# Gate and up products of the last stage as three fp16 products instead of one fp32 product

## The chip, the cores and the metric

The kernel runs on one core of one Trainium2 chip. The metric is the device time of one launch in microseconds (us); lower is better. Before the change the median of three runs is 945.73 us (944.59 to 948.35). "Before" is the kernel without the change, "after" the one with it.

## The reference, cut to what matters

A pre-norm decoder block over two sequences of 512 tokens of width 1024: a first attention with sign weights, a second attention (16 heads of 16 features, causal) inside a block that keeps four channels per feature, and a dense layer with adapters. The change touches the middle of the second block:

```
mlp_in = rat_read(hidden_states, mlp_read_w, g, b, 2)        # layer-normed reads
g_in, u_in = mlp_in[..., :H], mlp_in[..., H:]                # H = 256
gate = einsum('bli,oi->blo', g_in, ctx[0])                   # 256 -> 1024
up   = einsum('bli,oi->blo', u_in, ctx[1])                   # 256 -> 1024
mlp_out = silu(gate) * up
hidden_states = rat_write(hidden_states, mlp_out, ...)
```

All inputs and outputs are fp32.

## The kernel before, in words

The 1024 tokens are 8 tiles of 128. Three stages matter here. The *second attention* (lines 1859 to 1920 on TensorE, 1033 to 1048 on ScalarE, 1402 to 1443 on VectorE) runs 8 rounds of 16 score tiles: TensorE makes scores (L1860), VectorE takes their maxima (L1406), TensorE makes them again shifted (L1904), ScalarE takes the exponential (L1037), GpSimd masks (L779), TensorE sums with the values (L1915). The *last stage* then handles the 8 token tiles one after the other, software-pipelined: in the round of tile i, the "first" half makes the write of the attention result of tile i, the read and the gate and up products of tile i; the "second" half makes the write of the MLP result of tile i-1; "dense" makes the dense layer of tile i-2.

Order on each engine is program order; waits are counting semaphores. In the round of tile i of the last stage:

- TensorE: `products_1` (L1942), `products_2` (L1949), the dense layer's pieces (L1988, L1992, L2041, L2048, L2069), the transposes `turn_state` (L1822, region_p) and `turn_read` (L1822, yn), the read (L2001), and `gate_up` (L2013): 32 fp32 products of 128x128 weights (`ctx_w`) with 128 columns of the turned read `ynT`, each of which the trace shows as two records.
- ScalarE: among others `read_turned` (L1055, four copies with scale and shift that make `ynT`), then `decays` (L1025) of the write of tile i-1, then `gate`: a table load (L1059), the tanh (L1061), a table load (L1062).
- GpSimd: `read_root_2` (L797), `write` of tile i-1: `write_a` (L766) and `write_h` (L771, which waits for `decays`), then `dense_root` (L801); the write of the next tile and `attended` (L756) follow.
- VectorE: the read's statistics and normalisation (L1531 to L1539), the write of tile i-1 (`write_end`: L1474 to L1499, where L1493 waits for `decays` and L1499 for `write_h`), `gated` (L1546, after the tanh; L1549, after the up product), `to_dense` (L1554 to L1563), then the write of the next tile with L1517 in it; its last instruction, L1499, releases `turn_state`.

Tiles 0 and 1 are handled ahead of the steady rounds (2 to 7); after them come two rounds without a "first" half.

Of the kernel before, what the change touches and what calls it, by code (L numbers as in the profile page):

```python
# [103 lines left out]
def build_program(nc, d, out):  # L104
    ctx = ExitStack()
    with ctx:
# [89 lines left out]
        ctx_w = region_w[:, _o:_o + 4 * M].rearrange("p (w k n) -> p w k n", w=2, k=2)  # L196
# [41 lines left out]
        h_0 = c_o[:, 0:D]  # L238
        h2T = ops[:, 4 * S:8 * S].bitcast(F32).rearrange("p (c n) -> p c n", c=KC)
# [55 lines left out]
        def run_rounds(eng, round_):  # L295
# [69 lines left out]
        y2_step, y2_rstd, y2n_ready = sem("y2_step"), sem("y2_rstd"), sem("y2n_ready")  # L365
        y2T_mm, y2T_ready, gu_mm, tanh_ready, mlp_ready = (sem(n) for n in (
            "y2T_mm", "y2T_ready", "gu_mm", "tanh_ready", "mlp_ready"))
        f_step, f_rstd, xf_ready = (sem(n) for n in ("f_step", "f_rstd", "xf_ready"))
# [280 lines left out]
        def _(pool):  # L649
# [148 lines left out]

            def dense_root(i):
                pool.wait_ge(f_step, 5 * i + 5)  # L800
                pool.tensor_tensor(rstd[:, 0, :], ves[:], minus_half[:, 0:1], ALU.pow).then_inc(f_rstd, 1)  # L801

            read_root_2(0)
            write(0, 1, h_in)
            attended(2)
            read_root_2(1)
            write(1, 0, h_0)
            dense_root(0)
            for i in range(2, NT + 1):
# [5 lines left out]
                write(1, i - 1, h_mid[(i - 1) % 2])  # L815
                dense_root(i - 1)
# [3 lines left out]
        def _(act):  # L820
# [209 lines left out]

            act.preload_act_table_set("natural_log_exp_and_others")
            for i in range(XI):
                for n, (kt, j) in enumerate(X_PROB_TILES):
                    if i > 0 and n % 8 == 0:
                        act.wait_ge(xpv_done, 2 * i - 1 + n // 8)
# [16 lines left out]
            def read_turned(i):  # L1052
                act.wait_ge(y2T_mm, i + 1)
                for n in range(4):
                    act.activation(ynT[:, n, :], psum[:, 7, n * P:(n + 1) * P], ACT.Identity,  # L1055
                                   scale=cols[:, g2 + n:g2 + n + 1], bias=cols[:, b2 + n:b2 + n + 1]).then_inc(y2T_ready, 1)

            def gate(i, bank):
                act.preload_act_table_set("exp_and_others")  # L1059
                act.wait_ge(gu_mm, 2 * i + 1)  # L1060
                act.activation(mlpT_f.rearrange("p (h n) -> p h n", h=2), psum[:, bank:bank + 2, :], ACT.Tanh, scale=0.5).then_inc(tanh_ready, 1)  # L1061
# [49 lines left out]
        def _(dve):  # L1111
# [300 lines left out]

            def x_invert(b):
# [87 lines left out]
            for i in range(XI):  # L1501
                for n in range(16):
# [5 lines left out]
                    if (i, n) == (5, HEAD_INVERT):  # L1508
                        x_invert(0)
            to_state(0, h_0)  # L1510
# [32 lines left out]
            def gated(i, bank=0):  # L1543
# [5 lines left out]
                dve.scalar_tensor_tensor(t2, t2, 0.5, psum[:, 6:8, :], ALU.mult, ALU.mult).then_inc(mlp_ready, 1)  # L1549
# [60 lines left out]
        def _(pe):  # L1610
# [397 lines left out]
            def gate_up(i, bank):  # L2008
                pe.wait_ge(y2T_ready, 4 * i + 4)
# [142 lines left out]
```

## Time and profile before

| what | us |
|---|---|
| median of 3 runs | 945.73 |
| the profiled execution, its time | 947.53 |
| its span, first to last instruction | 945.8 |
| TensorE busy | 834.6 (88%) |
| VectorE busy | 648.4 (69%) |
| ScalarE busy | 418.0 (44%) |
| GpSimd busy | 305.9 (32%) |

The mean granted clock of TensorE is 0.934 of its full 2.4 GHz. The second attention lies between about 530 and 629 us of the span, the last stage from there to the end; the steady rounds begin their gate and up products at 705.99, 741.94, 777.88, and so on to 885.57 us, 35.9 us apart. PE is TensorE, PEld its weight loads, DVE VectorE, ACT ScalarE, POOL GpSimd.

### The profile page before, as it was taken

Reading aid. Unit: us, or ns where it says so; the run is one execution under the profiler, and the core shown is the slowest. Engines: PE = TensorE matmul, PEld = TensorE weight load, DVE = VectorE, ACT = ScalarE, POOL = GpSimd, SP = SyncE. Lnnn points to the kernel's source line nnn. Section 1 sums busy time; section 2 is a strip of 40 time slices with the busy share of each in tenths; the row PEclk is TensorE's granted clock in tenths of the full one; section 3 lists DMA queues with packets and bytes.
Section 4 is the critical chain, followed back from the end, with each engine's and each line's share of the span. In section 5 each row is a group of like instructions: output and inputs, shape, how many; then the busy total and the mean of one; then the engine's idle time right before and its main releaser. Section 6 shows DMA issues by size and latency. Waiting matters only on the chain.

```text
span 945.8 us, 15035 instructions
## 1 busy us (share of the span) xinstructions
PE 834.6 (88%) x5594; PEld 450.7 (48%) x5594; DVE 648.4 (69%) x1348; ACT 418.0 (44%) x819; POOL 305.9 (32%) x297
## 2 busy tenths in 40 slices
PE   4899689999999999899996778877799999999977
PEld 2675233333343333356664323236556656656633
DVE  7865367787887874467786667435678778679661
ACT  4466415676676767223343356533232332332310
POOL 2000004676676767310100135342232232232210
PEclk9899799999999999999997578768799999999997
DMA  8664522141322222111225431110001001001011
GB/s 329 235 231 137 167 73 90 60 111 47 108 79 77 88 67 96 57 45 42 79 68 167 182 97 59 47 43 17 1 1 47 16 30 45 10 35 34 7 38 45
DMA packets 75625, 75.78 MB, mean 80 GB/s; under 512 B 37493, under 2 KB 63877, under 8 KB 74918
## 3 DMA queue, kind: packets, MB, share of 16 engines
q1 hardware_dynamic: 74998, 68.77, 23.8%
q10 hardware_dynamic: 560, 6.12, 1.7%
q8 instruction: 41, 0.67, 0.3%
q14 instruction: 26, 0.21, 0.1%
HBM read 53.56 MB, written 21.04 MB: 79 GB/s over the span
## 4 chain that ended last, share of the span: by engine, by line
PE 67%; DVE 11%; ACT 7%; DMA 5%; SPq 4%; issue 4%; POOL 2%; POOLq 0%; DVEq 0%; ACTq 0%; PEldq 0%
PE psum L1625 6%; PE psum L1707 6%; PE psum L2013 6%; PE psum L1988 5%; PE psum L1758 5%; PE psum L1747 5%; PE psum L1949 4%; PE psum L1815 4%; PE psum L1822 3%; PE psum L1768 3%; PE psum L1915 3%; DMA ops<-q_scr 2%; SPq L536 2%; PE psum L1893 2%; PE psum L2001 2%
## 5 line engine op out<-in xcount | busy, mean ns | idle before, releaser
L1271 DVE TENSOR_REDUCE m_neg<-psum 128x1 f32<-128x512 f32 x256 | 164.5, 682 | 43.6 <-PE psum L1707 41.6
L911 ACT ACTIVATE region_x<-psum 128x512 f32<-128x512 f32 x256 | 140.8, 596 | 64.0 <-PE psum L1747 63.8
L679 POOL TENSOR_TENSOR region_p<-region_x 128x2048 f32<-128x2048 f32 x32 | 145.3, 4539 | 42.0 <-ACT region_x L911 25.7
L1707 PE MATMUL psum<-ops 96*128 96x512 f16 x256 | 97.0, 387 | 13.1 <-DMA ops<-q_scr 11.8
L1747 PE MATMUL psum<-ops 98*128 98x512 f16 x256 | 95.7, 381 | 1.7 <-ACT region_x L911 1.5
L1625 PE MATMUL psum<-region_x,region_w 128*128 128x512 f16 x320 | 77.0, 398 | 3.0 <-ACT region_w L849 3.0
L1707 PEld LDWEIGHTS psum<-ops 96*128 96x128 f16 x256 | 24.8, 97 | 93.5 <-DVE m_neg L1271 64.0
L2013 PE MATMUL psum<-ynT,region_w 128*128 128x128 f32 x512 | 63.5, 288 | 6.3 <-ACT ynT L1055 6.3
L1758 PE MATMUL psum<-region_x,v_g 128*32 128x512 f32 x512 | 67.8, 604 | 0.0
L2013 PEld LDWEIGHTS psum<-ynT,region_w 128*128 128x128 f32 x512 | 61.9, 203 | 10.0 <-ACT ynT L1055 10.0
L1815 PE MATMUL psum<-sign_o_all,region_a 128*128 128x512 f16 x256 | 60.2, 387 | 4.3 <-DVE region_p L1338 2.8
L1988 PE MATMUL psum<-region_a,c_o 128*128 128x512 f16 x256 | 59.3, 386 | 0.0
L1037 ACT ACTIVATE region_p<-psum 128x512 f32<-128x512 f32 (+2 forms) x96 | 39.2, 462 | 39.4 <-PE psum L1904 38.9
L1625 PEld LDWEIGHTS psum<-region_x,region_w 128*128 128x128 f16 x320 | 32.5, 102 | 45.7 <-issue 9.4
L1406 DVE CUSTOM_DVE_ANT_0 c_o<-psum,v_g 128x128 f32<-128x128 f32 (+3 forms) x86 | 39.2, 482 | 16.0 <-PE psum L1860 15.8
L779 POOL TENSOR_SCALAR_AFFINE_SELECT region_p<-region_p 128x128 f32<-128x128 f32 x96 | 27.9, 306 | 65.4 <-ACT region_p L1037 63.9
L1860 PE MATMUL psum<-ops 48*128 48x128 f16 (+3 forms) x128 | 36.9, 364 | 10.0 <-DVE m_neg L1406 8.5
L1949 PE MATMUL psum<-region_s,region_w 128*128 128x376 f32 x128 | 44.1, 490 | 1.5 <-DVE region_w L1549 1.5
L1904 PE MATMUL psum<-ops 50*128 50x384 f16 (+3 forms) x128 | 35.8, 367 | 10.6 <-ACT region_p L1037 6.0
L766 POOL TENSOR_TENSOR region_w<-sp_b 128x768 f32<-128x768 f32 x16 | 25.9, 1619 | 53.9 <-DVE sp_b L1474 53.9
L1815 PEld LDWEIGHTS psum<-sign_o_all,region_a 128*128 128x128 f16 x256 | 25.3, 100 | 31.8 <-DVE region_p L1338 3.0
L1988 PEld LDWEIGHTS psum<-region_a,c_o 128*128 128x128 f16 x256 | 24.8, 100 | 30.4 <-issue 4.3
(236 smaller groups left out, 1485.4 us busy)
## 6 DMA issues: line engine op xcount, KB each, us to landing
ops<-q_scr SPq DMA_DIRECT2D x48, 128.0 KB, 2.6
region_a<-in_x SPq DMA_DIRECT2D x8, 512.0 KB, 8.5
region_a<-in_w_q SPq DMA_DIRECT2D x8, 512.0 KB, 7.1
region_w<-in_w_o SPq DMA_DIRECT2D x8, 512.0 KB, 4.0
region_w<-in_kern SPq DMA_DIRECT2D x16, 256.0 KB, 2.9
kern_scr<-region_w SPq DMA_DIRECT2D x32, 128.0 KB, 1.9
region_p<-in_x SPq DMA_DIRECT2D x8, 512.0 KB, 3.6
region_a<-kern_scr ACTq DMA_DIRECT2D x1, 4096.0 KB
```

The source lines that it names most:

```text
L679: pool.tensor_tensor(pair_sum[:, n], prob_a[:, 2 * n], prob_a[:, 2 * n + 1], ALU.add).then_inc(pair_ready, 1)
L911: act.activation(prob_a[:, kt, j, :], psum[:, (0, 4, 5)[(16 * i + n) % 3], :], ACT.Exp, scale=A_SCALE).then_inc(p_ready, 1)
L1037: act.activation(prob_x[kt][:, j, :], psum[:, 4 + (16 * i + n) % 3, 0:S - kt * P], ACT.Exp, scale=X_SCALE).then_inc(xp_ready, 1)
L1271: dve.tensor_reduce(m_neg[:, i % 3, n:n + 1], psum[:, 1 + (16 * i + n) % 3, :], AX_X, ALU.max, negate=True).then_inc(s_max, 1)
L1625: mm = pe.matmul(psum[:, bank, 0:width], *((x[:, c, tokens], w) if swap else (w, x[:, c, tokens])), start=(c == 0 and part == 0), stop=(c ...
L1707: pe.matmul(psum[:, 1 + (16 * i + n) % 3, :], qa_op[u][0:A_MAX, j, qt * P:(qt + 1) * P], k_op[u][0:A_MAX, :], start=True, stop=True).then_ ...
L1747: pe.matmul(psum[:, (0, 4, 5)[(16 * i + n) % 3], :], k_op[u][0:A_ROWS, kt * P:(kt + 1) * P], qa_op[u][0:A_ROWS, j, :], start=True, stop=Tr ...
L1758: mm = pe.matmul(psum[j * 32:(j + 1) * 32, 6, :], v_g[:, i % 3, kt, :], prob_a[:, kt, j, :], start=(kt == 0), stop=(kt == QT - 1))
L1815: mm = pe.matmul(psum[:, h, :], (o_in_hi, o_in_lo)[n % 2][:, n // 2, ds(i * P, P)], sign_o[:, n // 2, h * 512:(h + 1) * 512], start=(n == ...
L1949: mm = pe.matmul(psum[:, 2, 0:N_W], mlpT[:, c, :], write2[:, c, :], start=(c == 0), stop=(c == KC - 1))
L1988: pe.matmul(psum[:, 4 + h, :], fT_hi[:, c, :], kern[:, w, c, h * 512:(h + 1) * 512], start=(c == 0 and w == 0), stop=False)
L2013: mm = pe.matmul(psum[:, at + f // 4, (f % 4) * P:(f % 4 + 1) * P], ctx_w[:, n, k, f * P:(f + 1) * P], ynT[:, 2 * n + k, :], start=(k == 0 ...
```

## The change

The weights of the gate and up products are split into two fp16 parts, high (times 64, rounded) and low (the rest), during rounds 2 to 5 of the second attention: 8 copies on ScalarE and 8 subtractions on VectorE of 128x512 each. The turned read is made in two fp16 parts as well: ScalarE writes the high part straight from PSUM (4 instructions) and then the fp32 form (the 4 that were there), and GpSimd subtracts the one from the other (`read_lo`, one instruction of 128x512). `gate_up` is then 96 fp16 products: 64 with the high part of the read (against the weights' high and low parts), and 32 with its low part (against the weights' high part). The semaphore for gate comes after the 16th of the last 32, that for up at the end. The factor 64 is taken out in the tanh's scale and in `gated`.

On GpSimd, in a steady round, `read_lo` stands behind both parts of the write. Before:

```order
L797 TENSOR_TENSOR rs<-ve,minus_half 128x2 [waits y2_step]
L766 TENSOR_TENSOR region_w<-sp_b 128x768 [waits sp_ready_2]
L771 TENSOR_TENSOR region_w<-region_p,region_w 128x768 [waits abar_ready_2]
L801 TENSOR_TENSOR rstd<-ves,minus_half 128x1 [waits f_step]
L766 TENSOR_TENSOR region_w<-sp_b 128x768 [waits sp_ready_1]
```

and after, at the same place:

```order
L801 TENSOR_TENSOR rs<-ve,minus_half 128x2 [waits y2_step]
L770 TENSOR_TENSOR region_w<-sp_b 128x768 [waits sp_ready_2]
L775 TENSOR_TENSOR region_w<-region_p,region_w 128x768 [waits abar_ready_2]
L806 TENSOR_TENSOR lo_st<-ynT,hi_st 128x512 [waits gu_mm,y2T_ready]
L810 TENSOR_TENSOR rstd<-ves,minus_half 128x1 [waits f_step]
L770 TENSOR_TENSOR region_w<-sp_b 128x768 [waits sp_ready_1]
```

L806 is new; `abar_ready_2` is what `decays` of the MLP write releases. On ScalarE the same round has this before (L1055 makes the turned read, L1025 is `decays`):

```order
L1055 ACTIVATE ynT<-psum,cols 128x128 [waits y2T_mm]
L1055 ACTIVATE ynT<-psum,cols 128x128 x3
L1025 ACTIVATE region_w<-region_w 128x768 [waits da_ready_2]
L1059 ACT_TABLE_LOAD
L1061 ACTIVATE region_w<-psum 128x1024 [waits gu_mm]
```

and this after:

```order
L1080 ACTIVATE hi_st<-psum,cols 128x128 [waits y2T_mm]
L1080 ACTIVATE hi_st<-psum,cols 128x128 x3
L1080 ACTIVATE ynT<-psum,cols 128x128 x4
L1038 ACTIVATE region_w<-region_w 128x768 [waits da_ready_2]
L1084 ACT_TABLE_LOAD
L1086 ACTIVATE region_w<-psum 128x1024 [waits gu_mm]
```

`decays` now stands behind four more instructions. On TensorE the two rows of `gate_up`, `L2013 ... [waits y2T_ready]` and its 31 followers, become 96 products; around the place where the low part of the read comes in, after:

```order
L2046 MATMUL psum<-hi_st,ops 128x128 x2
L2046 MATMUL psum<-hi_st,region_w 128x128 x2
L2046 MATMUL psum<-lo_st,ops 128x128 [waits y2_lo_ready]
L2046 MATMUL psum<-lo_st,region_w 128x128
L2046 MATMUL psum<-lo_st,ops 128x128
```

The row with `y2_lo_ready` is the 65th product; the wait is new. The diff, cut to its core:

```diff
@@ -193,7 +193,8 @@
...
         ctx_parts = region_w[:, _o:_o + 4 * M].rearrange("p (w n) -> p w n", w=4)
-        ctx_w = region_w[:, _o:_o + 4 * M].rearrange("p (w k n) -> p w k n", w=2, k=2)
+        _ctx = [ops[:, XI * 2 * S:(XI + 2) * 2 * S], ctx_parts[:, 0, :].bitcast(F16), ops[:, (XI + 2) * 2 * S:(XI + 4) * 2 * S], ctx_parts[:, 1, :].bitcast(F16)]
+        ctx_hi, ctx_lo = ([c[:, n * M:(n + 1) * M] for c in _ctx] for n in range(2))
@@ -236,6 +237,7 @@
...
         h_0 = c_o[:, 0:D]
+        y2_hi, y2_lo = (t[:].rearrange("p (c n) -> p c n", c=4) for t in (hi_st, lo_st))
@@ -363,8 +365,10 @@
...
         y2_step, y2_rstd, y2n_ready = sem("y2_step"), sem("y2_rstd"), sem("y2n_ready")
+        CTX_TILES = {(i + 2, n): (i, n // 8) for i in range(4) for n in (3, 11)}
...
             "y2T_mm", "y2T_ready", "gu_mm", "tanh_ready", "mlp_ready"))
+        ctx_hi_ready, ctx_lo_ready, y2_lo_ready = (sem(n) for n in ("ctx_hi_ready", "ctx_lo_ready", "y2_lo_ready"))
@@ -796,15 +800,22 @@
...
 
+            def read_lo(i):
+                pool.wait_ge(y2T_ready, 8 * i + 8)
+                pool.wait_ge(gu_mm, 2 * i)
+                pool.tensor_tensor(y2_lo, ynT[:, 0:4, :], y2_hi, ALU.subtract).then_inc(y2_lo_ready, 1)
+
...
             read_root_2(0)
+            read_lo(0)
...
             write(1, 0, h_0)
+            read_lo(1)
@@ -813,6 +824,8 @@
...
                 write(1, i - 1, h_mid[(i - 1) % 2])
+                if i < NT:
+                    read_lo(i)
@@ -1028,9 +1041,20 @@
...
 
+            def split_ctx_hi(c, h):
+                if (c, h) == (0, 0):
+                    act.wait_ge(xw_loaded, 16 * 6)
+                if h == 0 and c % 2 == 0:
+                    act.wait_ge(xst_mm, 16 * (c + 2))
+                if c % 2 == 1:
+                    act.wait_ge(ctx_lo_ready, 2 * (c // 2) + 2)
+                act.activation(ctx_hi[c][:, h * 512:(h + 1) * 512], ctx_parts[:, c, h * 512:(h + 1) * 512], ACT.Copy, scale=F_GAIN).then_inc(ctx_hi_ready, 1)
+
...
                 for n, (kt, j) in enumerate(X_PROB_TILES):
+                    if (i, n) in CTX_TILES:
+                        split_ctx_hi(*CTX_TILES[i, n])
@@ -1051,14 +1075,15 @@
...
                 act.wait_ge(y2T_mm, i + 1)
-                for n in range(4):
-                    act.activation(ynT[:, n, :], psum[:, 7, n * P:(n + 1) * P], ACT.Identity,
-                                   scale=cols[:, g2 + n:g2 + n + 1], bias=cols[:, b2 + n:b2 + n + 1]).then_inc(y2T_ready, 1)
+                for to in (y2_hi, ynT):
+                    for n in range(4):
+                        act.activation(to[:, n, :], psum[:, 7, n * P:(n + 1) * P], ACT.Identity,
+                                       scale=cols[:, g2 + n:g2 + n + 1], bias=cols[:, b2 + n:b2 + n + 1]).then_inc(y2T_ready, 1)
...
                 act.wait_ge(gu_mm, 2 * i + 1)
-                act.activation(mlpT_f.rearrange("p (h n) -> p h n", h=2), psum[:, bank:bank + 2, :], ACT.Tanh, scale=0.5).then_inc(tanh_ready, 1)
+                act.activation(mlpT_f.rearrange("p (h n) -> p h n", h=2), psum[:, bank:bank + 2, :], ACT.Tanh, scale=0.5 / F_GAIN).then_inc(tanh_ready, 1)
@@ -1410,6 +1435,12 @@
...
 
+            def split_ctx_lo(c, h):
+                dve.wait_ge(ctx_hi_ready, 2 * c + h + 1)
+                part = slice(h * 512, (h + 1) * 512)
+                dve.scalar_tensor_tensor(ctx_lo[c][:, part], ctx_parts[:, c, part], F_GAIN, ctx_hi[c][:, part],
+                                         ALU.mult, ALU.subtract).then_inc(ctx_lo_ready, 1)
+
@@ -1507,6 +1538,8 @@
...
                         x_invert(0)
+                    if (i, n - 4) in CTX_TILES:
+                        split_ctx_lo(*CTX_TILES[i, n - 4])
@@ -1546,7 +1579,7 @@
...
                 dve.wait_ge(gu_mm, 2 * i + 2)
-                dve.scalar_tensor_tensor(t2, t2, 0.5, psum[:, 6:8, :], ALU.mult, ALU.mult).then_inc(mlp_ready, 1)
+                dve.scalar_tensor_tensor(t2, t2, 0.5 / F_GAIN ** 2, psum[:, 6:8, :], ALU.mult, ALU.mult).then_inc(mlp_ready, 1)
@@ -2006,12 +2039,24 @@
...
             def gate_up(i, bank):
-                pe.wait_ge(y2T_ready, 4 * i + 4)
-                for n, at in ((0, bank), (1, 6)):
+                pe.wait_ge(y2T_ready, 8 * i + 4)
+
+                def product(n, f, k, w, y, start, stop):
+                    at = (bank, 6)[n] + f // 4
+                    return pe.matmul(psum[:, at, (f % 4) * P:(f % 4 + 1) * P], w[2 * n + k][:, f * P:(f + 1) * P], y[:, 2 * n + k, :], start=start, stop=stop)
+
+                for n in range(2):
+                    for f in range(KC):
+                        if (n, f) == (1, KC // 2):
+                            pe.wait_ge(y2T_ready, 8 * i + 8)
+                        for k in range(2):
+                            product(n, f, k, ctx_hi, y2_hi, f % 4 == 0 and k == 0, False)
+                            product(n, f, k, ctx_lo, y2_hi, False, False)
+                pe.wait_ge(y2_lo_ready, i + 1)
+                for n in range(2):
...
                         for k in range(2):
-                            mm = pe.matmul(psum[:, at + f // 4, (f % 4) * P:(f % 4 + 1) * P], ctx_w[:, n, k, f * P:(f + 1) * P], ynT[:, 2 * n + k, :],
-                                           start=(k == 0), stop=(k == 1))
+                            mm = product(n, f, k, ctx_hi, y2_lo, False, f % 4 == 3 and k == 1)
@@ -2072,6 +2117,7 @@
...
             pe.wait_ge(made, 21)
+            pe.wait_ge(ctx_lo_ready, 8)
```

## Rows read from the trace of the kernel before

**Rows 1.** The page, part 1: busy us (share), instructions.

```profile
PE 834.6 (88%) x5594; PEld 450.7 (48%) x5594; DVE 648.4 (69%) x1348; ACT 418.0 (44%) x819; POOL 305.9 (32%) x297
```

**Rows 2.** Windows: length, busy of PE, PEld, DVE, ACT, POOL; PEclk, DMA share, GB/s.

```profile
740.00:892.00 152.00, 144.21 (x886) 96.42 (x884) 120.94 (x198) 51.03 (x92) 40.72 (x29) 1.00 0.10 26
```

**Rows 3.** Timeline of TensorE, a steady round: start, length, instruction, [idle before].

```profile
741.94 7.41 PE L2013 MATMUL psum<-ynT,region_w 128*128 128x128 f32 x64 [0.52 <-ACT ynT L1055]
749.19 0.81 PE L1992 MATMUL psum<-region_a,c_o 128*128 128x512 f16 x3
749.83 1.88 PE L2069 MATMUL psum<-region_w 65*128 65x512 f32 x4
...
768.19 1.04 PE L1822 MATMUL psum<-ident,region_p 128*128 128x128 f32 x8
```

**Rows 4.** Timeline of TensorE, sixteen fp16 products of 128 columns.

```profile
761.79 1.05 PE L2041 MATMUL psum<-c_o,region_w 128*64 128x128 f16 x16 [1.25 <-ACT c_o L1029]
```

**Rows 5.** Timeline of ScalarE, the same steady round.

```profile
740.38 1.51 ACT L1055 ACTIVATE ynT<-psum,cols 128x128 f32<-128x128 f32 x4 [5.15 <-PE psum L1822]
741.76 0.85 ACT L1025 ACTIVATE region_w<-region_w 128x768 f32<-128x768 f32 x1
...
745.81 1.02 ACT L1061 ACTIVATE region_w<-psum 128x1024 f32<-128x1024 f32 x1 [1.89 <-PE psum L2013]
```

**Rows 6.** GpSimd: timeline of two writes.

```profile
670.96 2.50 POOL L771 TENSOR_TENSOR region_w<-c_o,region_w 128x768 f32<-128x768 f32 x1 [1.47 <-ACT region_w L1025]
...
742.70 2.04 POOL L771 TENSOR_TENSOR region_w<-region_p,region_w 128x768 f32<-128x768 f32 x1 [1.02 <-ACT region_w L1025]
```

**Rows 7.** Groups of instructions by shape: busy us, mean ns, idle before.

```profile
L683 POOL TENSOR_TENSOR region_a<-region_w,region_a 128x512 f16<-128x512 f32 x14 | 16.3, 1161 | 24.0 <-ACT region_a L920 24.0
```

**Rows 8.** Timeline of VectorE: the write of tile 0, then the steady round.

```profile
670.91 0.96 DVE L1493 SCALAR_TENSOR_TENSOR region_w<-region_w 128x768 f32<-128x768 f32 x1
...
749.46 1.22 DVE L1549 SCALAR_TENSOR_TENSOR region_w<-region_w,psum 128x1024 f32<-128x1024 f32 x1 [0.79 <-PE psum L2013]
...
763.02 2.02 DVE L1493 SCALAR_TENSOR_TENSOR region_w<-region_w 128x768 f32<-128x768 f32 x1
...
766.06 0.96 DVE L1499 TENSOR_TENSOR region_p<-region_w 128x768 f32<-128x768 f32 x1
```

**Rows 9.** Timeline of TensorE, two idle gaps in dense work, and a window behind one.

```profile
387.80 3.63 PE L1815 MATMUL psum<-sign_o_all,region_a 128*128 128x512 f16 x16 [1.44 <-PEq L1828]
399.72 8.77 PE L1815 MATMUL psum<-sign_o_all,region_a 128*128 128x512 f16 x32 [2.83 <-DVE region_p L1338]
```

**Rows 10.** Windows, behind the second of these gaps (columns as in rows 2).

```profile
401.00:404.00 3.00, 3.00 (x8) 1.06 (x7) 2.24 (x6) 0.00 (x0) 0.55 (x1) 0.50 0.45 147
```

**Rows 11.** Groups by shape: splits of 128x512 weights in the first attention.

```profile
L924 ACT ACTIVATE region_w<-region_w 128x512 f16<-128x512 f32 x16 | 10.0, 624 | 2.2 <-DMA region_w<-in_kern 2.2
...
L1300 DVE SCALAR_TENSOR_TENSOR region_w<-region_w 128x512 f16<-128x512 f32 x16 | 11.4, 713 | 2.5 <-ACT region_w L924 2.5
```

**Rows 12.** Timeline of the second attention: idle of ScalarE and of VectorE.

```profile
578.34 0.49 ACT L1037 ACTIVATE region_p<-psum 128x384 f32<-128x384 f32 x1 [2.24 <-PE psum L1904]
...
572.26 0.42 DVE L1406 CUSTOM_DVE_ANT_0 c_o<-psum,v_g 128x256 f32<-128x256 f32 x1 [0.69 <-PE psum L1860]
...
578.12 0.29 DVE L1406 CUSTOM_DVE_ANT_0 c_o<-psum,v_g 128x128 f32<-128x128 f32 x1 [1.42 <-PE psum L1860]
```

**Rows 13.** Timeline, start of the last stage (DVE, PE).

```profile
642.50 0.47 DVE L1474 SCALAR_TENSOR_TENSOR sp_b<-region_w 128x304 f32<-128x304 f32 x1 [1.62 <-ACT region_w L1021]
...
652.93 5.32 PE L1949 MATMUL psum<-region_s,region_w 128*128 128x376 f32 x16 [1.46 <-DVE region_w L1549]
```

**Rows 14.** Timeline of TensorE behind the last gate and up products.

```profile
895.18 5.22 PE L1949 MATMUL psum<-region_s,region_w 128*128 128x376 f32 x16
...
922.22 1.97 PE L1822 MATMUL psum<-ident,region_p 128*128 128x128 f32 x8 [5.21 <-DVE region_p L1563]
...
925.36 1.91 PE L2041 MATMUL psum<-c_o,region_w 128*64 128x128 f16 x16 [1.17 <-ACT c_o L1029]
```

## The prediction, on record before the changed kernel ran

> **What bounds the kernel now.** I read the page first: TensorE is busy 88% of the span [rows 1]. Then the stage windows: over 152 us of steady rounds of the last stage it is busy 144.2 us, at full granted clock (1.00, that is 2.4 GHz) [rows 2]. So there a microsecond taken from TensorE counts only as far as nothing else comes late, and each wait put in front of it counts at once. Third, the timelines of the four engines through one steady round. I measure from G, the start of the gate and up products (741.94). They run from G to G+7.25, where the next instruction starts at 749.19 [rows 3]; ScalarE's four copies end at G [rows 5]; the tanh starts at G+3.87; VectorE ends L1549 at 750.68, G+8.74, and its last instruction, L1499, at 767.02 [rows 8], while TensorE asks for the result at 768.19 [rows 3]. VectorE has thus 1.15 us of room; TensorE sets the period, and the change adds a wait in its queue.
>
> **The products alone.** Sixteen fp16 products of 128 columns take 1.05 us [rows 4]. The end of such a run holds about 0.16 us in which the next may already go (7.41 against 7.25 in rows 3), so one costs (1.05 - 0.16)/16 = 56 ns. 96 cost 5.4 us against 7.25, 1.85 less per tile. The stationary side in rows 4 is 64 columns wide, here it is 128; the nearest rows with 128 are those of the old products, 7.41/64 = 116 ns a record. I take 56 and keep 116 as the other end.
>
> The Trainium skill ("TensorE: Matmul & The Clock Gate", Back-to-back issue gap) gives about 81 ns for a 128-column product with its own weight load, against 56 for an isolated one. No run here shows 128 weight columns at this size, and rows 4 are nearer to 56; by 81 the 64 products would end at G+5.2 and the whole at G+8.5, an estimate, with a much shorter wait in between and about the same total as my sum.
>
> **When the low part of the read is there.** Step by step, in a steady round:
> - ScalarE's four copies take 1.38 us from 740.38 to the start of L1025 at 741.76 [rows 5]; four more put that start at G+1.2 and its end (0.85) at G+2.1. The high part is ready at G, as the fp32 form was.
> - GpSimd's L771 waits for L1025. So does VectorE's L1493, which is free by then. This pair was released together once before: VectorE took 0.96 us and GpSimd 2.50 [rows 6, 8], while elsewhere it needs 2.04. So L771 ends at G+2.1+0.1+2.5 = G+4.7.
> - `read_lo` stands behind it and has the shape of L683, 1.16 us [rows 7]: ready at G+5.9.
>
> The skill ("SBUF — State Buffer", Who interferes with whom) says that only the port pair shared by VectorE and GpSimd collides, and that the lock is exclusive. The trace agrees: 2.50 us is about 0.96 + 1.6.
>
> **TensorE.** After 64 products it stands at G+3.6 and waits 2.3 us for G+5.9; 32 more take 1.8: the end is G+7.7 instead of G+7.25, +0.45. The 1.85 gained has turned into the wait. Queued behind the waiting product are L1992, L2069 and the next tile's `products_1`; all come 0.45 later. Over five periods between the six steady rounds: **+2.3**. As a lower bound (L771 at 2.04, nothing blocked) the low part is there at G+5.3 and the end is G+7.1: -0.15 a round.
>
> **VectorE.** The gate semaphore now comes 16 products after the low part: G+5.9+0.9+0.16 = G+7.0. The tanh (1.02, rows 5) ends at G+8.1, the two of `gated` (1.22 each) at G+10.6 instead of G+8.74: +1.9. It has 1.15 of room, and part of the delay is taken back at L1493 of the next write: at 763.02 it took 2.02 us, blocked by GpSimd's L771; coming later it meets less of it, up to 1.06 less. What is left of 1.9 is at most the 0.45 that TensorE is late anyway. **0** here.
>
> **Behind the last tile** no `products_1` stands between: L1949 starts at 895.18 = G+9.6 [rows 14] and waits for `gated`, now G+10.6: **+1.0**.
>
> **Start of the stage.** In the round of tile 0, GpSimd makes the low part at once, but L1474 waits for ScalarE's L1021 (642.50, idle 1.62) [rows 13], which stands behind the four new copies: +1.4 down to L1949 at 652.93. TensorE's products end earlier and its successor starts later, so its idle of 1.46 there becomes some 5 us. Behind the one gap of that size, 5.21 us, the granted clock was at its lower level: the eight transposes took 1.97 against 1.04 and L2041 1.91 against 1.05 [rows 14, 3, 4], 1.8 in sum. So **+3.2**; bounds 1.4 (clock held) to 4.5. In the round of tile 1 the wait for VectorE ends as late as before: 0.
>
> **Clock in the steady rounds.** The new gap is 2.3 us. A gap of 1.44 in dense work left 16 products at 3.63; after one of 2.83 the clock read 0.50 (1.2 GHz) and 32 of them took 8.77 instead of 7.1, 1.7 lost [rows 9, 10]. 2.3 lies between and nearer to the latter. I take three falls in six rounds: **+5.1**; bounds 0 and 10.2.
>
> **Second attention.** ScalarE gets 8 copies of 0.62 and VectorE 8 subtractions of 0.71 [rows 11]. ScalarE's stand where it waits 2.24 us for TensorE's sums [rows 12] (or half that, at the other place) and cost nothing; without that cover, 8 x 0.62 = 5.0. VectorE's stand behind its 8th and 16th tile of a round; its idle comes only a few tiles later (0.69 and 1.42, rows 12), so a score product that needs the next maximum waits some: I take 0.2 of 0.71 each, **+1.6**, bounds 0 and 5.7.
>
> **Sum.** 2.3 + 0 + 1.0 + 3.2 + 5.1 + 1.6 = 13.2 on the profiled execution's 947.53 gives 960.7. That execution stands 1.8 above the median of 945.73, so the median after is **959**, 1.4% slower. Without falls of the clock it is 954, with six 964.
>
> **Rivals.**
> - *The low part comes in time, faster.* Place: GpSimd in front of `read_lo`. The copies are complete at G+1.4; were GpSimd free then, the part would be there at G+2.6, before G+3.6, and TensorE would keep 1.85 in each of five periods: -9.3, with start and attention (+1.4, +1.6) 945.7 - 6.3 = about 939. It decides from the point where L771 ends before G+2.4, 2.3 us sooner than I work out. For it: GpSimd is idle most of the time (32%). Against: the order on GpSimd and ScalarE. Chance 0.07.
> - *The wait is short and the clock holds.* The lower bounds together: the part at G+5.3, gap 1.7, no fall, attention free: 945.7 + 1.4 + 0.5 - 0.8 = 947; up to 950 with a part of the rest. Chance 0.14.
> - *The products cost nearer to 116 ns.* 64 end at G+7.4, after the low part, so no gap and no fall; all 96 at G+11.1, +3.9 a round: 5 x 3.9 + 4 behind the last + 1.4 + 1.6 = 26.5, 972. For it: each product has a weight load of its own. Against: rows 4 have that too. Chance 0.07.
> - *The forecast*, a wait of about 2 us with or without falls, 951 to 968: 0.72.
>
> **Numbers.** Range 948 to 969. Half a per cent, 4.7 us, is about what a measurement of this kernel can tell. Faster by more: 0.07. Within: 0.14 (the second rival). Slower by more: 0.79.
>
> **What would show it.** In the profile after: a wait of TensorE for GpSimd's subtraction, 2.3 us, before the 65th product in each steady round; products 56 ns apart before it; L771 at about 2.5 us right in front of the subtraction; L1546 waiting for the tanh, which starts at G+7; periods of 36.4 us, and about 1.7 more where the granted clock reads 0.50 behind the gap; L1949 of tile 0 starting 1.4 later relative to its G. Wrong would be: no wait at the 65th product (the first rival), a spacing over 80 ns, or a second attention longer by more than 5 us.

## The result, and the profile after

The changed kernel takes 964.75 us (median of 4 runs, 962.37 to 966.32), the kernel before in the same session 945.16 (944.45 to 948.35): a ratio of 1.0173, 95% interval 1.0134 to 1.0212. A later session of six runs gave 1.0215 (1.0176 to 1.0254). The change makes the kernel about 2% slower. The profiled execution has a span of 964.0 us against 945.8, so 18.2 us more are to be found. A *fall*, below, is a stretch in which TensorE's granted clock reads 0.50 in the middle of dense work.

The first row of the page shows 256 matmuls more than [rows 1] and hardly more busy time:

```profile
PE 836.0 (87%) x5850; PEld 443.9 (46%) x5850; DVE 650.5 (67%) x1356; ACT 433.8 (45%) x859; POOL 319.4 (33%) x305
```

The same window of steady rounds as in [rows 2]: TensorE is busy for 136.4 us of 152 instead of 144.2, and its granted clock is 0.97 on average. It idles more, and some of its work runs slower.

```profile
740.00:892.00 152.00, 136.42 (x966) 86.08 (x965) 111.64 (x193) 51.28 (x101) 44.09 (x31) 0.97 0.10 26
```

One steady round, G = 751.12, where G is the start of the gate and up products as in the prediction. These rows are the counterparts of [rows 3, 5, 6, 8]. Line numbers are those of the changed kernel: L2046 the products, L1080 the copies, L1038 the decays, L775 `write_h`, which was L771, L806 `read_lo`, L1086 the tanh. In the kernels of the experiments the same instructions stand a few lines off (the products at L2045 in e_early, at L2049 in e_swapst). TensorE:

```profile
751.12 0.28 PE L2046 MATMUL psum<-hi_st,ops 128*128 128x128 f16 x2 [0.52 <-ACT hi_st L1080]
...
756.95 0.23 PE L2046 MATMUL psum<-lo_st,ops 128*128 128x128 f16 x1 [2.08 <-POOL lo_st L806]
757.02 0.22 PE L2046 MATMUL psum<-lo_st,region_w 128*128 128x128 f16 x1
...
758.16 0.31 PE L2046 MATMUL psum<-lo_st,region_w 128*128 128x128 f16 x1
758.26 0.31 PE L2046 MATMUL psum<-lo_st,ops 128*128 128x128 f16 x1
...
759.76 1.45 PE L2025 MATMUL psum<-region_a,c_o 128*128 128x512 f16 x3
```

ScalarE, VectorE and GpSimd in the same round:

```profile
749.56 1.50 ACT L1080 ACTIVATE hi_st<-psum,cols 128x128 f16<-128x128 f32 x4 [5.15 <-PE psum L1855]
750.95 1.52 ACT L1080 ACTIVATE ynT<-psum,cols 128x128 f32<-128x128 f32 x4
752.32 0.88 ACT L1038 ACTIVATE region_w<-region_w 128x768 f32<-128x768 f32 x1
...
758.29 1.02 ACT L1086 ACTIVATE region_w<-psum 128x1024 f32<-128x1024 f32 x1 [3.79 <-PE psum L2046]
...
753.23 0.96 DVE L1524 SCALAR_TENSOR_TENSOR region_w<-region_w 128x768 f32<-128x768 f32 x1 [0.83 <-ACT region_w L1038]
...
753.28 2.51 POOL L775 TENSOR_TENSOR region_w<-region_p,region_w 128x768 f32<-128x768 f32 x1 [2.42 <-ACT region_w L1038]
755.74 1.16 POOL L806 TENSOR_TENSOR lo_st<-ynT,hi_st 128x512 f16<-128x512 f32 x1
```

Read down this is the chain of the prediction: four copies more, so the decays start at G+1.2; the store released with VectorE's L1524 takes 2.51; the low part ends at G+5.8; TensorE has stood still for 2.08 us. Then something else begins: from 757.6 on the low products are 0.107 us apart instead of 0.056, and three products of 512 columns take 1.45 instead of 0.81 [rows 3]. The granted clock there is its lower level, 1.2 GHz. It falls a second time later in the round, at 774.7, under sixteen products of 512 columns. They come 1.6 us after a wait of 1.25 us for ScalarE's copies, which stands at the same place in the kernel before [rows 4]; I call it the old wait. The two windows, columns as in [rows 2]:

```profile
757.75:761.00 3.25, 3.25 (x24) 2.65 (x23) 1.61 (x2) 2.31 (x2) 0.00 (x0) 0.50 0.00 0
774.75:778.00 3.25, 3.25 (x9) 1.10 (x8) 3.18 (x3) 0.00 (x0) 2.10 (x2) 0.50 0.00 0
```

The start of the stage (counterparts of [rows 13]): VectorE's L1505 waits for the logarithm behind eight copies, and TensorE's L1982 waits 5.16 us and then takes 7.98 us for what took 5.32.

```profile
645.98 0.70 DVE L1505 SCALAR_TENSOR_TENSOR sp_b<-region_w 128x304 f32<-128x304 f32 x1 [3.20 <-ACT region_w L1034]
...
656.66 7.98 PE L1982 MATMUL psum<-region_s,region_w 128*128 128x376 f32 x16 [5.16 <-DVE region_w L1582]
```

G of each tile, read from the two traces, and the distance to the next G:

| | G of tile 0 | 0 to 1 | 1 to 2 | 2 to 3 | 3 to 4 | 4 to 5 | 5 to 6 | 6 to 7 | G of 7 to the end |
|---|---|---|---|---|---|---|---|---|---|
| before | 641.69 | 28.51 | 35.79 | 35.95 | 35.94 | 35.95 | 35.95 | 35.79 | 60.2 |
| after | 643.77 | 33.34 | 36.03 | 37.98 | 39.66 | 36.32 | 36.31 | 37.82 | 62.8 |

So the 18.2 us are: 2.1 ahead of the stage (2.2 are there already at the first maximum of the second attention, 496.85 against 494.63, ahead of everything that the change touches; from there to G of tile 0 it is 0.1 less), 4.8 in the round of tile 0, 0.2 in that of tile 1, 8.5 in five periods, 2.5 behind the last G. A period without a fall is 36.32, 0.37 more than before. A fall adds about 1.66 (37.98 - 36.32), two 3.34. There are five: four in the periods (6.65 us) and one at 907.8 behind the last tile. Four of them (720.1, 757.6, 870.3, 907.8) begin within 1.2 us of the end of the new wait, the fifth (774.7) behind the old one. From G of tile 0 to the end the changed kernel takes 16.1 us more than the kernel before, and 16.4 in the profile of its repetition.

### The profile page after: what moved, and what is told of

Its sections match the earlier page's. It is cut to its first block, busy times and chain, and to the rows that moved or that the text cites. A ratio compares the mean times of both kernels' runs of the same rounds, so it can differ in the third digit from the quotient of the medians.

```text
span 964.0 us, 15616 instructions
## 1 busy us (share of the span) xinstructions
PE 836.0 (87%) x5850; PEld 443.9 (46%) x5850; DVE 650.5 (67%) x1356; ACT 433.8 (45%) x859; POOL 319.4 (33%) x305
## 4 chain that ended last, share of the span: by engine, by line
PE 62%; DVE 12%; ACT 6%; issue 6%; POOL 5%; DMA 5%; SPq 4%; POOLq 0%; DVEq 0%; ACTq 0%; PEldq 0%
PE psum L1658 6%; PE psum L1740 6%; PE psum L1791 5%; PE psum L1982 5%; PE psum L1780 5%; PE psum L1848 4%; PE psum L2021 4%; PE psum L1855 3%; PE psum L1801 3%; PE psum L1948 3%; DMA ops<-q_scr 2%; PE psum L2046 2%; PE psum L1926 2%; SPq L540 2%; POOL region_w L775 2%
## 5 line engine op out<-in xcount | busy, mean ns | idle before, releaser
L1848 PE MATMUL psum<-sign_o_all,region_a 128*128 128x512 f16 x256 | 60.2, 387 | 4.3 <-DVE region_p L1363 2.8
L2021 PE MATMUL psum<-region_a,c_o 128*128 128x512 f16 x256 | 61.5, 396 | 0.0
L1982 PE MATMUL psum<-region_s,region_w 128*128 128x376 f32 x128 | 46.7, 513 | 5.2 <-DVE region_w L1582 5.2
L775 POOL TENSOR_TENSOR region_w<-region_p,region_w 128x768 f32<-128x768 f32 x14 | 30.7, 2190 | 26.0 <-ACT region_w L1038 26.0
L2046 PE MATMUL psum<-hi_st,ops 128*128 128x128 f16 x256 | 33.7, 237 | 6.3 <-ACT hi_st L1080 6.3
```

What stands on the lines that cost most here:

```text
L775: pool.tensor_tensor(b.h_a.rearrange("p (s r c) -> p s r c", s=HS, r=RH), h3[:, :, :, 0:C - 1], a3, ALU.mult).then_inc(W["ha_ready"][k], 1)
L1848: mm = pe.matmul(psum[:, h, :], (o_in_hi, o_in_lo)[n % 2][:, n // 2, ds(i * P, P)], sign_o[:, n // 2, h * 512:(h + 1) * 512], start=(n == ...
L1982: mm = pe.matmul(psum[:, 2, 0:N_W], mlpT[:, c, :], write2[:, c, :], start=(c == 0), stop=(c == KC - 1))
L2021: pe.matmul(psum[:, 4 + h, :], fT_hi[:, c, :], kern[:, w, c, h * 512:(h + 1) * 512], start=(c == 0 and w == 0), stop=False)
L2046: return pe.matmul(psum[:, at, (f % 4) * P:(f % 4 + 1) * P], w[2 * n + k][:, f * P:(f + 1) * P], y[:, 2 * n + k, :], start=start, stop=stop)
```

## The experiments

Each ratio is against the kernel before in its own session, with its 95% interval. "Falls" are stretches at the lower clock from G of tile 2 up to the end of the work that follows the last G at full clock; before has none in its profile. "New" are those that begin behind the wait for the low part, "old" those behind the old wait. The last four columns of each row come from one profile.

| kernel | median us (before) | ratio | G0 to G1 | steady period without a fall | falls, new | falls, old |
|---|---|---|---|---|---|---|
| after | 964.75 (945.16) | 1.0173 (1.0134 to 1.0212) | 33.3 | 36.32 | 4 | 1 |
| r_after, the same again | 965.24 (946.59) | 1.0215 (1.0176 to 1.0254) | 33.3 | 36.31 | 4 | 1 |
| e_warm | 957.79 (948.14) | 1.0103 (1.0058 to 1.0148) | 31.7 | 36.33 | 0 | 0 |
| r_warm, the same again | 959.90 (946.59) | 1.0135 (1.0103 to 1.0166) | 33.3 | 36.33 | 0 | 1 |
| e_swapst | 950.94 (948.07) | 1.0026 (1.0006 to 1.0046) | 33.3 | 35.17 | 0 | 1 |
| e_fill | 958.79 (948.07) | 1.0106 (1.0072 to 1.0140) | 33.3 | 35.85 (the last one) | 0 | 4 |
| e_early | 943.08 (948.14) | 0.9956 (0.9924 to 0.9987) | 33.3 | 34.07 | no wait | 0 |
| e_first | 942.29 (948.07) | 0.9926 (0.9896 to 0.9955) | 31.9 | 34.07 | no wait | 0 |
| e_first_warm | 939.56 (948.07) | 0.9914 (0.9884 to 0.9944) | 29.4 | 34.07 | no wait | 1 |
| e_splits | 949.10 (948.14) | 1.0017 (0.9982 to 1.0052) | 28.5 | 35.94 | no wait | 0 |
| e_copies | 951.65 (948.14) | 1.0032 (1.0009 to 1.0054) | 33.1 | 35.95 | no wait | 1 |

### e_early: the low part ahead of the store

```diff
+            def write(k, i, h, b=wr, lo=None):
                 write_a(k, i, a3)
+                if lo is not None:
+                    read_lo(lo)
                 write_h(k, i, h3, a3, b)
-            write(1, i - 1, h_mid[(i - 1) % 2])
-            if i < NT:
-                read_lo(i)
+            write(1, i - 1, h_mid[(i - 1) % 2], lo=i if i < NT else None)
```

> The changed kernel with one thing moved: on GpSimd the reading of the low part stands ahead of the 2.5 us store of the high part (write_h) instead of behind it. Theory T (the five steady periods lose 0.37 us each by the 2.1 to 2.3 us in which TensorE waits for the low part, and four falls of the clock behind that wait take the rest): the low part is there at about G+2.6, before the 65th product at G+3.6, no wait in front of it, gate_up ends at about G+5.5, the granted clock stays 1.00 in the steady rounds, the periods are 35.0 to 35.5 us against 36.3 to 39.7 in the changed kernel, and the time is 944 to 952 us against 964.7. Rival R1 (the falls come from something else, the products' own load above all): the wait goes but falls of the clock stay, periods near 37, time 957 to 962. Rival R2 (the store of the high part is what sets the round, through the attention products that read it): moving it behind the read makes it 1.2 us later and the time stays at 962 to 967.

Measured: 943.08, 0.9956 of before and some 20 us under the changed kernel, 1 us under the expected 944 to 952. The order of GpSimd (first fence) gives the low part at G+2.6, and TensorE (second fence, G = 777.86) runs its 96 products without a stop, 5.37 us:

```profile
779.27 1.16 POOL L808 TENSOR_TENSOR lo_st<-ynT,hi_st 128x512 f16<-128x512 f32 x1 [1.69 <-ACT ynT L1079]
780.40 2.45 POOL L777 TENSOR_TENSOR region_w<-region_p,region_w 128x768 f32<-128x768 f32 x1
```

```profile
777.86 0.29 PE L2045 MATMUL psum<-hi_st,ops 128*128 128x128 f16 x2 [0.52 <-ACT hi_st L1079]
...
781.44 0.22 PE L2045 MATMUL psum<-lo_st,ops 128*128 128x128 f16 x1
...
783.23 0.81 PE L2024 MATMUL psum<-region_a,c_o 128*128 128x512 f16 x3
```

The period is 34.07, 1.88 under before: the whole saving of the products. I had expected some of it to be lost on VectorE (35.0 to 35.5); none was. R2 falls. Its premise was too large, though: the store starts at G+2.54 against G+2.16, 0.4 us later and not 1.2, because it stood waiting for the decays before. That 0.4 us costs nothing. R1 falls here too: with the wait gone, this profile has no fall.

### e_warm and r_warm: the gap filled with idle products

```diff
+                for m in range(fill):              # 40 in rounds 1 to 7
+                    pe.matmul(psum[:, 3, 0:P], ctx_hi[0][:, 0:P], y2_hi[:, 0, :], start=True, stop=True)
                 pe.wait_ge(y2_lo_ready, i + 1)
```

> The changed kernel with 40 products more in each of rounds 1 to 7, between the 64 products of the high part and those of the low part, into a bank of PSUM whose content nobody reads; they compute nothing that is used. The wait for the low part stays as long, but TensorE is busy in it. Theory T: the first product of the low part starts as before at about G+5.9, the clock no longer falls behind it, the five steady periods are 36.3 us each (now 36.0 to 39.7), and the time is 956 to 960 us against 964.7. Rival R1 (the falls don't come from the gap): the clock falls as often as before or more often, time 963 to 970. Rival R2 (the 40 products end later than the low part comes): each round is longer by what they pass G+5.9, 0.1 to 0.5 us, which would show as products without a wait.

> The changed kernel once more, beside its twin with the gap filled (r_warm) in one session, since the first runs of the two were taken apart and only four of the changed kernel were timed. Theory T (falls of the granted clock behind the wait, about 1.7 us each, three to five in the six rounds behind the first two and the tail): 1.7% over the kernel before, 0.6 to 0.8% (6 to 8 us) over r_warm, and in the profile periods of 36.3 us, longer ones only where the clock reads 0.50. Rival (the falls in the first profile were chance): all periods 36.3, and the same time as r_warm, 1.0% over the kernel before.

> The kernel of e_warm once more: the changed kernel with 40 products in the wait of rounds 1 to 7 whose results nobody reads. Theory T: 1.0% over the kernel before, no fall of the clock in the steady rounds, periods 36.3 us each. Rival (chance): a few falls here too, and the time of r_after.

These two keep the low part late and take away only TensorE's idleness. The low products still start at G+5.83 (G = 786.74):

```profile
791.34 1.17 POOL L806 TENSOR_TENSOR lo_st<-ynT,hi_st 128x512 f16<-128x512 f32 x1
```

```profile
786.74 0.29 PE L2046 MATMUL psum<-hi_st,ops 128*128 128x128 f16 x2 [0.52 <-ACT hi_st L1080]
...
792.57 0.23 PE L2046 MATMUL psum<-lo_st,ops 128*128 128x128 f16 x1
...
794.37 0.81 PE L2025 MATMUL psum<-region_a,c_o 128*128 128x512 f16 x3
```

Two profiles with the gap show five falls each, four of them right behind it. Two with it filled show none and one; the one (773.9 in r_warm, where I had expected none) stands behind the old wait, none at the filled gap. In one session the changed kernel stands at 1.0215 and its filled twin at 1.0135, intervals apart, 0.8% or 7.6 us between them; the medians differ by 5.3. Four to five falls of 1.66 are 6.6 to 8.3. So the clock behind the gap is a cost of its own, and the rival (chance) falls. What the twin keeps over before is the wait (0.37 a round) and the start; in its two profiles another 4 to 5 us lie ahead of the stage, where executions differ anyway (below).

### e_swapst: a shorter wait

```diff
                 if first:
-                    read_turned(i)
+                    read_turned(i, (0,))     # fp16 copies
                 if second:
                     decays(1, i - 1)
+                if first:
+                    read_turned(i, (1,))     # fp32 copies
```

> The changed kernel with the order of ScalarE alone turned in rounds 1 to 7: the decays (0.88 us) stand ahead of the four fp32 copies. The order of GpSimd stays, low part behind the high part's store. Both then end 1.4 us earlier: the low part is there at about G+4.5 instead of G+5.9, TensorE waits 0.7 to 0.9 us instead of 2.1 to 2.3. Theory T (it is the wait and the clock behind it): GATE_UP ends at G+6.2, the steady periods are 34.9 us, no or at most one fall of the clock in them, time 948 to 954 us. Rival (falls come as often with a wait of 0.9 us): 1.7 us more for each, 954 to 960 us.

Measured: wait 0.93, period 35.17 (0.27 more than I wrote), one fall, 950.94, inside the expected 948 to 954. GpSimd and TensorE (G = 820.04):

```profile
820.79 2.03 POOL L775 TENSOR_TENSOR region_w<-region_p,region_w 128x768 f32<-128x768 f32 x1 [1.02 <-ACT region_w L1038]
822.78 1.87 POOL L806 TENSOR_TENSOR lo_st<-ynT,hi_st 128x512 f16<-128x512 f32 x1
```

```profile
824.71 0.23 PE L2049 MATMUL psum<-lo_st,ops 128*128 128x128 f16 x1 [0.93 <-POOL lo_st L806]
```

The order of ScalarE alone takes away over half of the wait, that of GpSimd (e_early) all of it. The low part is 0.2 us later than I wrote: the store is 0.5 shorter than in the changed kernel (2.03), but the subtraction, beside VectorE's work, now takes 1.87 instead of 1.16. No fall stands behind the wait of 0.93; the one there is, at 733.7, stands behind the old wait. One profile does not prove that number, but the time agrees with it.

### e_fill: useful work in the gap

```diff
+                between()      # dense_lo(1, 5..7) and the adapter's products, from behind gate_up
                 pe.wait_ge(y2_lo_ready, i + 1)
```

> The changed kernel with the last 2.36 us of TensorE's work on the tile before (three products of 512 columns and the two of the adapter with their bias) moved from behind GATE_UP into its middle, between the products of the high part and those of the low part; GpSimd's and ScalarE's order stays. The wait of 2.1 us is filled with useful work, the low products start as before at about G+5.9 to G+6.0. Theory T with TensorE as the engine that bounds the round: what is moved away from behind GATE_UP comes off the round in full, periods 34.0 to 34.3 us against 36.3 to 39.7, no fall of the clock, time 942 to 948 us, like e_early. Rival (the round is bound by the tanh behind GATE_UP and VectorE behind it, which stay where they are): periods 36.3, only the falls go, 956 to 960 us.

The theory missed: 958.79, in the rival's 956 to 960. The gap is filled as planned (low products at G+5.95), but the period without a fall is 35.85 (there is only one, the last), not 34.1, and each of four rounds has a fall. TensorE in the round with G = 783.85:

```profile
787.43 0.81 PE L2025 MATMUL psum<-region_a,c_o 128*128 128x512 f16 x3
788.08 1.88 PE L2113 MATMUL psum<-region_w 65*128 65x512 f32 x4
...
793.30 1.50 PE L1975 MATMUL psum<-region_s,v_g 128*128 128x368 f32 x4 [1.56 <-DVE region_w L1579]
```

The 2.36 us of work moved forward had covered another wait: L1975 writes bank 0 of PSUM, which L1579 of VectorE reads behind the tanh. Without that cover TensorE waits 1.56 us there. The rival's mechanism (the round is bound by the tanh behind GATE_UP) holds, its period of 36.3 nearly. And falls came in another place, 21.5 us behind G, at 767.8 and 805.4 for two of the four, in the dense work behind the old wait:

```profile
768.25:771.25 3.00, 3.00 (x8) 1.03 (x7) 2.97 (x4) 0.00 (x0) 2.77 (x2) 0.50 0.00 0
805.75:808.75 3.00, 3.00 (x9) 1.06 (x7) 2.96 (x4) 0.00 (x0) 2.91 (x2) 0.50 0.00 0
```

The old wait stands in the kernel before [rows 4] and is followed by no fall there. But it can be followed by one with no other wait added to the steady rounds: one round of e_first_warm (first fence) and one of e_copies (second) show it, where sixteen products of 512 columns take 5.31 us instead of 3.63.

```profile
798.27 1.05 PE L2085 MATMUL psum<-c_o,region_w 128*64 128x128 f16 x16 [1.25 <-ACT c_o L1040]
799.25 0.69 PE L1991 MATMUL psum<-v_all,region_s 8*128 8x256 f32 x2
799.88 5.31 PE L2020 MATMUL psum<-region_a,c_o 128*128 128x512 f16 x16
```

```profile
836.56 1.05 PE L2047 MATMUL psum<-c_o,region_w 128*64 128x128 f16 x16 [1.25 <-ACT c_o L1030]
837.54 0.69 PE L1963 MATMUL psum<-v_all,region_s 8*128 8x256 f32 x2
838.17 5.31 PE L1992 MATMUL psum<-region_a,c_o 128*128 128x512 f16 x16
```

So falls have two places in this kernel. Those right behind the wait for the low part stand in the two profiles in which it is an idle 2.08 us, and in none of the other ten. Those behind the old wait come at most once in a profile, with and without the new one, except in e_fill with its four. Whether e_fill's own gap of 1.56 us, which ends 12 us ahead of the fall, brings them is not shown: five rounds have that gap and four a fall, and the rounds are also laid out differently. What picks the round is left open.

### e_splits and e_copies: parts of the change alone, on the kernel before

```diff
+                    if (i, n) in CTX_TILES:
+                        split_ctx_hi(*CTX_TILES[i, n])      # e_splits; the subtraction on VectorE likewise
```

> The kernel before with the 16 splits of weights alone added to the second attention, on the same engines and at the same places as in the change; their results go to space that nobody reads. By the traces of the two kernels the second attention lasts the same in both, so theory T expects 0 to +1.6 us on 945.5, 945 to 947. The rival, the upper bound of the prediction for these splits: +5.7, 951.

```diff
+                for n in range(4):                          # e_copies
+                    act.activation(y2_hi[:, n, :], psum[:, 7, n * P:(n + 1) * P], ACT.Identity, ...)
```

> The kernel before with one part of the change alone: each reading of the tile is copied by ScalarE once more into an fp16 tile, in pieces of a quarter, in front of the decays (four copies more in each round, read by nobody), and GATE_UP waits for its input at the second place as in the change; the products stay fp32. Theory T: in the steady rounds the four copies put the decays and with them the 2.5 us store about 1.4 us later, which costs 0 to 0.2 us a round as VectorE has room, and at the start of the stage 1.4 us; 945.5 + 1.4 to 3 = 947 to 948.5. Rival: the delay of the decays costs VectorE its full 1.4 us in each of seven rounds, 955.

The splits: G of tile 0 at 641.34 against 641.69 in the profiles, the time +0.2% with an interval of -0.2 to +0.5%. They cost about nothing; the upper bound of 5.7 is excluded in the profile and just so by the times.

The copies: the steady periods stay at 35.95, so the later decays cost nothing there; the rival (1.4 in each of seven rounds) falls. But G0 to G1 is 33.1, 4.6 of the 4.8 us that the changed kernel loses there, and the round of tile 1 takes 1.1 more (36.90), as the lower clock lasts until 6.2 us behind its G instead of 3.8. In the round of tile 0 TensorE waits 2.80 and then runs at the lower clock:

```profile
651.49 8.35 PE L1953 MATMUL psum<-region_s,region_w 128*128 128x376 f32 x16 [2.80 <-DVE region_w L1553]
```

The loss of 3.5 us by medians is above my 1.4 to 3, which its interval (0.9 to 5.1) still holds. The loss at the start is thus the placement of four copies, with or without fp16 products.

### e_first and e_first_warm: the round of tile 0

```diff
-            read_turned(0)
+            read_turned(0, (0,))
             log_part(0, 1)
+            read_turned(0, (1,))
             decays(0, 1)
 ...
-            read_lo(0)
-            write(0, 1, h_in)
+            write(0, 1, h_in, lo=0)
```

e_first_warm adds, on TensorE:

```diff
             gate_up(0, 2)
+            for m in range(64):
+                pe.matmul(psum[:, 4, 0:P], ctx_hi[0][:, 0:P], y2_hi[:, 0, :], start=True, stop=True)
```

> The kernel of e_early (low part read before the high part's store) with the round of tile 0 mended: on ScalarE its two logarithms stand ahead of its four fp32 copies, and on GpSimd the reading of its low part stands behind write_a instead of in front of it. In e_early G of tile 1 comes 33.3 us behind G of tile 0, in the kernel before 28.5. Theory T1 (1.6 us of the 4.8 are the fp32 and the fp16 copies on the way from the logarithms to VectorE's subtraction, the rest is TensorE at half clock behind its 5.2 us wait for that subtraction): the subtraction ends 1.6 us earlier behind G, at G+11.2; TensorE still waits 3.6 us, so the clock can still fall: G of tile 1 at G+28.5 to G+31.7, the time 938 to 942 us against 943.1. Rival R1 (the loss is all in the clock, which does not care): G of tile 1 at G+33, time 943. Both against 948.1 us of the kernel before in the same session.

> The kernel of e_first with 64 products more behind GATE_UP of tile 0 alone, whose results nobody reads: TensorE is busy for 3.6 us of the wait for VectorE's subtraction. Theory T1: the 16 products of the next group, 7.98 us at half clock in the changed kernel, take 5.3 us, G of tile 1 comes at G+28.5 and the time is 1 to 3.2 us under that of e_first. Rival: the clock at this place is low for what came before (the second attention), G of tile 1 as in e_first, and the time within 0.5 us of it.

In e_first L1981 starts 0.75 earlier behind G than in e_early (12.12 against 12.87), not 1.6, and G1 comes 1.4 earlier. VectorE shows where the rest is: two operations of 0.41 and 0.63 now meet the subtraction and the store of GpSimd and last 1 us longer each, while L1523, which met the store in e_early (2.45), gets 1 us back (1.44):

```profile
651.71 1.41 DVE L1512 TENSOR_TENSOR region_w<-sp_b,region_w 128x256 f32<-128x256 f32 x1
653.15 0.42 DVE L1515 TENSOR_TENSOR region_w<-region_w,psum 128x256 f32<-128x256 f32 x1
653.61 1.58 DVE L1517 TENSOR_TENSOR region_p<-region_p,region_w 128x256 f32<-128x256 f32 x1
```

```profile
651.69 1.15 POOL L808 TENSOR_TENSOR lo_st<-ynT,hi_st 128x512 f16<-128x512 f32 x1
652.80 1.91 POOL L777 TENSOR_TENSOR region_w<-region_p,region_w 128x768 f32<-128x768 f32 x1
```

Of the 1.4 us only the 0.75 are surely the edit's. How much of the work behind the wait runs at the lower clock differs from one execution to the next. Seven profiles have the code of the changed kernel in this round: the sixteen products took 7.96 to 8.30 us in six of them, with G1 at G0+33.3, and 6.92 in e_warm, with G1 at G0+31.7. By the times e_first is not told from e_early either.

The clock is tested by the pair. e_first, then e_first_warm, TensorE behind the wait:

```profile
660.89 7.01 PE L1981 MATMUL psum<-region_s,region_w 128*128 128x376 f32 x16 [3.81 <-DVE region_w L1581]
```

```profile
659.77 5.32 PE L1981 MATMUL psum<-region_s,region_w 128*128 128x376 f32 x16 [0.41 <-DVE region_w L1581]
```

Both start at G+12.1. With 64 unused products in the wait the sixteen take 5.32, as in the kernel before and in no profile with that wait left empty, and G1 comes 2.5 us earlier. By the times the two are 2.7 apart in median, but the intervals of their ratios overlap: the profile shows it, the times alone do not. e_first_warm has the lowest median, 0.9% under before; e_first, without products for nothing, is 0.7% under.

## Why the prediction was right, step by step

The forecast (959, range 948 to 969, slower) held: 964.75. Direction and mechanism were right, and two terms were too small, the falls and the start. Its terms, against what was measured:

| term | predicted | measured |
|---|---|---|
| product of 128 columns | 56 ns | 0.111 us between pairs: 56 ns (neither the 81 nor the 116 that it weighed) |
| low part there | G+5.9 | G+5.8 |
| wait before the 65th product | 2.3 | 2.08 |
| five steady periods | +2.3 | +1.85 (5 x 0.37; L2025 starts at G+7.63 in e_warm, at G+7.25 before) |
| VectorE in them | 0 | 0 (the 0.37 are all TensorE's; e_copies: period 35.95) |
| behind the last tile | +1.0 | +0.9 (e_warm: L1982 at G+10.53, before G+9.61) |
| start of the stage | +3.2 | +4.8 (3.2 in e_warm, with the same code there) |
| falls of the clock, steady rounds | +5.1 (3 of 6) | +8.3 (5; four at the new wait, one at the old) |
| second attention | +1.6 | -0.1 (e_splits: G of tile 0 0.35 earlier) |
| round of tile 1 | 0 | +0.2 |
| sum | 13.2 | 18.2, of which 2.1 ahead of the stage |

*The mechanism* is shown from both sides: taking the low part forward (e_early) removes the wait, filling it (e_warm and r_warm) leaves the low part as late as it was and takes away the falls behind it.

*Most off in size: the clock.* I counted falls by the length of the new wait, between two gaps of the dense work [rows 9, 10], took three of six and allowed at most one for each. Both profiles of the changed kernel show four behind the new wait. The fifth stands 24 us behind G, behind the old wait of 1.25. I had read that wait as harmless, since no fall follows it in the one profile before; in seven of the eleven other profiles at least one does, two of them without any new wait in the steady rounds. The price of one, 1.7, was right.

*The start.* The first half is right (1.4 predicted, subtraction 1.64 later behind G). For the clock I took 1.8, from the transposes and the small products in [rows 14]. But here the first work behind the wait is 16 products of 376 columns, and they alone lost 2.66 (7.98 against 5.32). L1992 lost another 0.5, as the next low stretch, which the kernel before has too, came over it. I should have priced the work that really follows the gap. Part of this is chance: e_warm, with the same code in this round, lost 3.2 in all.

*Second attention.* Its 16 splits cost nothing: I should have weighed the idle of VectorE a few tiles later [rows 12] as full cover.

*Ahead of the second attention:* 2.1 us that the change did not bring. G of tile 0 comes at 643.77 in the profile of the changed kernel, but at 639.90 in that of its repetition, 1.8 us before that of the kernel before. It comes at 640.36 in e_early and at 648.77 in e_first, whose code is the same up to there. Where these executions differ is open. In 28 executions of the kernel before in one session the longer ones mostly had the lower mean clock (spans 938.8 to 951.8, clocks 0.943 to 0.920, correlation -0.71).

*The rivals.* The first (in time, faster) needed the low part before G+3.6. e_early makes that true: 0.44% under before, where the rival said 0.7% (939), and most of the difference is the start, 4.8 where the rival counted 1.4. The second (short wait, clock holds, 947 to 950, or 0.1 to 0.5% over before) is nearly e_swapst: 0.26% over before at a wait of 0.93. The third, 116 ns a product, is out.

## What to carry to other kernels

- A part that is made behind a long store on a shared engine comes as late as the store: here exchanging two instructions on GpSimd was worth 20 us of 965, and turned a loss of 2% into a gain of 0.4%. Before splitting an operand in two, work out when each half is there.
- Price a new gap of TensorE twice: the gap, and the work behind it at half clock, by the instructions that really stand there. One profile without a fall behind a wait does not make that wait harmless: look at several before you count on it.
- Before filling a gap with work from elsewhere, ask what that work covers where it stands (e_fill).

## What the runs showed of the hardware that was not expected

- An idle gap of TensorE of 2.08 us a round was followed by a stretch at 1.2 GHz in four of six rounds, in both profiles of the changed kernel. Behind a gap of 0.93 there was none, and none where the 2.08 were filled with products that nobody needs. Work for nothing was worth about 0.8% of the time here.
- A wait of 1.25 us that every round of every kernel here has was followed by such a stretch in no steady round of five profiles, in one round of six others, and in four of e_fill. The stretch does not begin at the wait but 1.7 to 2.0 us after its end, in dense work.
- An operation of 0.41 us on VectorE took 1.41 beside GpSimd's subtraction of 1.15 (e_first), and GpSimd's own 1.16 became 1.87 beside VectorE's (e_swapst): both sides of a collision of the two can pay.
